# Half of the weight-slice loads of the ternary quantization moved from the SP queue to the ACT queue

## Chip, cores and metric

One Trainium2 chip, 8 cores, one program on all of them. Each core takes half of one of four sequences (2048 tokens and a few at the edges). The metric is the device time in microseconds of the slowest core, as the median over runs.

## The reference

A recurrent attention-like layer and a quantized feed-forward layer, each followed by a layer norm. Cut to what matters here:

```python
# layer 1, x: (4, 4096, 1024)
xp = x @ W_in + b_in
Bx = (xp @ W_B + b_B) @ B_mat            # 16 states
ig, fg = sigmoid(xp @ W_ig + b_ig), sigmoid(xp @ W_fg + b_fg)
h_t = fg_t * h_{t-1} + ig_t * Bx_t       # scan over 4096 tokens
y = tanh(hs @ C_mat + xp @ W_D + b_D) @ W_out + b_out + xp
x = layernorm(x + layernorm(y) * gamma + beta)
# layer 2: w1 (4096, 1024), w2 (1024, 4096)
def weight_quant(w):                     # ternary
    scale = 1.0 / clip(mean(abs(w)), 1e-5)
    return clip(round(w * scale), -1, 1) / scale
def act_quant(x): ...                    # to 8 bits, a scale for each token
h = silu(depthwise_conv(act_quant(x) @ weight_quant(w1).T))
x = layernorm(x + act_quant(h) @ weight_quant(w2).T)
```

The change lies in `weight_quant`: every core computes the mean of |w| of both matrices and then their ternary form.

## The kernel before

The kernel keeps a list of operations in program order (`Prog`). Each operation names its engine and the regions it reads and writes; `finalize_and_emit` works out the semaphore waits and writes one instruction stream for each engine, in program order. A wait stands in the stream of the engine that issues the operation, a DMA's too, so a DMA issued from ACT waits, and makes ACT wait, at its place among ACT's own computations. `load` (L242) issues on the SP queue unless it is told another; `store` (L246) issues on the ACT queue. SP computes nothing.

There are three stages with a barrier between them.

**Stage A** (to about 640 us). First the weights of the gates are folded (to 125 us). Then a loop over 16 *gate slices* of 256 tokens: an SP load of `xgf` (1 MB, two buffers), ACT makes its bf16 part `xgh` (L594), DVE the remainder `xgl` (L598), PE does 24 matmuls into `ps_g`, ACT evicts three gates (L615, L619, L623). At the end of each gate slice, `pump_p1(9)` puts in nine steps of the generator `tern_all`, which quantizes w1 and w2. After the loop come the scan and what the barrier waits for.

`tern_all` has four parts, 98 steps in all:

- `tern_pass1` over w1: 16 items of 128 x 2048 floats (1 MB each) and a step for the mean
- `tern_pass1` over w2: 32 items of 128 x 1024 floats (0.5 MB) and a step for the mean
- `tern_pass2` over w1: 16 items, the same data loaded again, and stored as bf16 (0.5 MB)
- `tern_pass2` over w2: 32 items, stored as bf16 (0.25 MB)

Item i uses load buffer `twf[i % 4]`, and scratch buffers `tu`, `tk16` and `tb` number i % 2. In pass 1 the sum of |w| of an even item is made by ACT (L447, into `tcol0`), that of an odd item by DVE (L452); after each, DVE adds it to a running sum (L460, L464), in order. In pass 2 an even item goes ACT `tu` (L533), DVE `tk16` (L537), ACT `tb` (L540), store from ACT (L247). An odd item goes DVE `tu` (L544), DVE `tk16` (L548), ACT `tb` (L551), store from ACT. The load of item i waits until item i - 4 has read its buffer. Since SP does nothing else, it issues a load as soon as that has happened, up to four items ahead of the computation.

With nine steps to a gate slice, pass 1 runs in gate slices 0 to 5 and pass 2 in gate slices 5 to 10. Slices 11 to 15 have no quantization in them.

**Stage B** (to about 1400 us) is the attention part, **stage C** the feed-forward part, which loads the ternary weights that stage A stored.

Of the kernel before, what the change touches and what calls it, by code (L numbers as in the profile page):

```python
# [184 lines left out]
def build_nc(debug=False):  # L185
# [150 lines left out]
    for fc in range(8):  # L336
# [3 lines left out]
        for j in range(8):  # L340
# [4 lines left out]
             i=ps_pre[:, po:po + 16], fc=fc:  # L345
# [91 lines left out]
    def tern_pass1(src, nrows, width, mean_out, mean_rg, tg,  # L437
                   ps_hbuf, ps_rg, scol):
        stag = f"tcol{scol}"
        slices = tern_slices(nrows, width)  # L440
        for i, (rc, c0, c1) in enumerate(slices):
            wv = c1 - c0
            pr = i % NTB
            twf, tu = twfs[pr], tus[pr]
            load(twf[:, 0:wv], src[rc * 128:(rc + 1) * 128, c0:c1], f"twf{pr}")
            if i % 2 == 0:
                p.op("ACT", lambda twf=twf, tu=tu, e=wv: A.activation(  # L447
                    tu[:, 0:e], twf[:, 0:e], AF.Abs, accum_out=tcol[:, 0:1]),
                     reads=(f"twf{pr}",), writes=(f"tu{pr % 2}", "tcol0"))
                acc, arg = "tcol0", 0  # L450
            else:
                p.op("DVE", lambda twf=twf, e=wv: V.tensor_reduce(  # L452
                    tcol[:, 3:4].rearrange("p (t o) -> p t o", o=1),
                    twf[:, 0:e].rearrange("p (t e) -> p t e", t=1),
                    AX, OP.add, apply_absolute_value=True),
                     reads=(f"twf{pr}",), writes=("tcol3",))
                acc, arg = "tcol3", 3
            ac = 6 + (i % 4)
            if i < 4:
                p.op("DVE", lambda ac=ac, a=arg: V.tensor_copy(  # L460
                    tcol[:, ac:ac + 1], tcol[:, a:a + 1]),
                     reads=(acc,), writes=(f"tcol{ac}",))
            else:
                p.op("DVE", lambda a=arg, ac=ac: V.tensor_add(  # L464
                    tcol[:, ac:ac + 1], tcol[:, ac:ac + 1], tcol[:, a:a + 1]),
                     reads=(acc, f"tcol{ac}"), writes=(f"tcol{ac}",))
            yield
        nun = len(slices)
        p.op("DVE", lambda: V.tensor_add(tcol[:, 6:7], tcol[:, 6:7],
                                         tcol[:, 7:8]),  # L470
             reads=("tcol6", "tcol7"), writes=("tcol6",))
        if nun > 2:
            p.op("DVE", lambda: V.tensor_add(tcol[:, 8:9], tcol[:, 8:9],
                                             tcol[:, 9:10]),
                 reads=("tcol8", "tcol9"), writes=("tcol8",))
            p.op("DVE", lambda: V.tensor_add(tcol[:, 6:7], tcol[:, 6:7],
                                             tcol[:, 8:9]),
                 reads=("tcol6", "tcol8"), writes=("tcol6",))
        p.op("DVE", lambda: V.tensor_scalar(tcol[:, 1:2], tcol[:, 6:7],
                                            1.0 / (nrows * 128 * width), None,  # L480
                                            OP.mult),
             reads=("tcol6",), writes=("tcol1",))
        mm("parsum" + tg, ps_hbuf[0:1, 0:1], s_onesc[:], tcol[:, 1:2],
           reads=("s_onesc", "tcol1"), wr=ps_rg, start=True, stop=True)
        p.op("DVE", lambda: V.tensor_copy(tcol[0:1, 1:2], ps_hbuf[0:1, 0:1]),
             reads=(ps_rg,), writes=("tcol1",))
        mm("parbc" + tg, ps_hbuf[0:128, 0:1], s_ones1[:], tcol[0:1, 1:2],
           reads=("s_ones1", "tcol1"), wr=ps_rg, start=True, stop=True)
        p.op("DVE", lambda: V.tensor_copy(tcol[:, 1:2], ps_hbuf[0:128, 0:1]),
             reads=(ps_rg,), writes=("tcol1",))  # L490
        p.op("DVE", lambda: V.tensor_scalar_max(mean_out[:], tcol[:, 1:2], 1e-5),
             reads=("tcol1",), writes=(mean_rg,))
        p.op("DVE", lambda mo=mean_out, sc=scol: V.reciprocal(
            tcol[:, sc:sc + 1], mo[:]),
             reads=(mean_rg,), writes=(stag,))
        yield

    def tern_pass2(src, dst_hbm, nrows, width, tg, scol):
        stag = f"tcol{scol}"
        slices = tern_slices(nrows, width)  # L500
        for i, (rc, c0, c1) in enumerate(slices):
            wv = c1 - c0
            pr = i % NTB
            twf, tu, tk16, tb = twfs[pr], tus[pr], tk16s[pr], tbs[pr]
            load(twf[:, 0:wv], src[rc * 128:(rc + 1) * 128, c0:c1], f"twf{pr}")
            if SAFE_ROUND:
                p.op("DVE", lambda twf=twf, tu=tu, e=wv: V.tensor_scalar(
                    tu[:, 0:e], twf[:, 0:e], tcol[:, scol:scol + 1], None,
                    OP.mult),
                     reads=(f"twf{pr}", stag), writes=(f"tu{pr % 2}",))  # L510
                p.op("DVE", lambda tu=tu, e=wv: V.tensor_copy(tk[:, 0:e],
                                                              tu[:, 0:e]),
                     reads=(f"tu{pr % 2}",), writes=("tk",))
                p.op("DVE", lambda tu=tu, e=wv: V.tensor_sub(trr[:, 0:e],
                                                             tu[:, 0:e],
                                                             tk[:, 0:e]),
                     reads=(f"tu{pr % 2}", "tk"), writes=("trr",))
                p.op("DVE", lambda e=wv: V.tensor_scalar(tcp[:, 0:e], trr[:, 0:e],
                                                         0.5, None, OP.is_gt),
                     reads=("trr",), writes=("tcp",))  # L520
                p.op("DVE", lambda tu=tu, e=wv: V.scalar_tensor_tensor(
                    tu[:, 0:e], trr[:, 0:e], -0.5, tcp[:, 0:e], OP.is_lt,
                    OP.subtract),
                     reads=("trr", "tcp"), writes=(f"tu{pr % 2}",))
                p.op("DVE", lambda tu=tu, e=wv: V.tensor_sub(tu[:, 0:e],
                                                             tk[:, 0:e],
                                                             tu[:, 0:e]),
                     reads=(f"tu{pr % 2}", "tk"), writes=(f"tu{pr % 2}",))
                p.op("DVE", lambda tu=tu, tb=tb, e=wv: V.tensor_scalar(
                    tb[:, 0:e], tu[:, 0:e], 1.0, -1.0, OP.min, OP.max),  # L530
                     reads=(f"tu{pr % 2}",), writes=(f"tb{pr % 2}",))
            elif i % 2 == 0:
                p.op("ACT", lambda twf=twf, tu=tu, e=wv: A.activation(  # L533
                    tu[:, 0:e], twf[:, 0:e], AF.Identity,
                    scale=tcol[:, scol:scol + 1]),
                     reads=(f"twf{pr}", stag), writes=(f"tu{pr % 2}",))
                p.op("DVE", lambda tu=tu, tk16=tk16, e=wv: V.tensor_scalar(  # L537
                    tk16[:, 0:e], tu[:, 0:e], 1.49, -1.49, OP.min, OP.max),
                     reads=(f"tu{pr % 2}",), writes=(f"tk16{pr % 2}",))
                p.op("ACT", lambda tk16=tk16, tb=tb, e=wv: A.activation(  # L540
                    tb[:, 0:e], tk16[:, 0:e], AF.Copy),
                     reads=(f"tk16{pr % 2}",), writes=(f"tb{pr % 2}",))
            else:
                p.op("DVE", lambda twf=twf, tu=tu, e=wv: V.tensor_scalar(  # L544
                    tu[:, 0:e], twf[:, 0:e], tcol[:, scol:scol + 1], 1.49,
                    OP.mult, OP.min),
                     reads=(f"twf{pr}", stag), writes=(f"tu{pr % 2}",))
                p.op("DVE", lambda tu=tu, tk16=tk16, e=wv: V.tensor_scalar(  # L548
                    tk16[:, 0:e], tu[:, 0:e], -1.49, None, OP.max),
                     reads=(f"tu{pr % 2}",), writes=(f"tk16{pr % 2}",))  # L550
                p.op("ACT", lambda tk16=tk16, tb=tb, e=wv: A.activation(  # L551
                    tb[:, 0:e], tk16[:, 0:e], AF.Copy),
                     reads=(f"tk16{pr % 2}",), writes=(f"tb{pr % 2}",))
            store(dst_hbm[rc * 128:(rc + 1) * 128, c0:c1], tb[:, 0:wv],
                  (f"tb{pr % 2}",), f"q{tg}{rc}_{c0}")
            yield
# [31 lines left out]
    for sl in range(T // GSL):  # L588
        c0 = sl * GSL
# [1027 lines left out]
```

How the kernel before makes its waits and increments, by code:

```python
                def body(handle, eng=eng, idxs=idxs):  # L164
                    for i in idxs:
                        o = ops[i]
                        for sh, val in waits_l[i]:
                            handle.wait_ge(sh, val)
                        instr = o["fn"]() if o["fn"] is not None else handle.nop()
                        if o["sem"] is not None:
                            instr.then_inc(o["sem"][1], 16 if o["dma"] else 1)
                    if eng == "SP":
                        for e2 in ENGINES:
                            if cnt.get(e2, 0):
                                handle.wait_ge(chain[e2], cnt[e2])
                        for j in range(NDMA):
                            if dcnt[j]:
                                handle.wait_ge(dpool[j], dcnt[j])
```

## Time and profile before

| | us |
|---|---|
| median of 2 runs | 2471.48 |
| the two runs | 2469.33, 2473.63 |
| the profiled execution | 2487.02 |
| its slowest core's span (core 7) | 2485.5 |
| shortest span of a core in it (core 2) | 2442.4 |

The profile is of one execution, on its slowest core. Busy over the whole span: PE 55%, DVE 45%, ACT 35%, POOL 5%. These are averages over three stages with different limits; the change touches stage A alone, so the rows that count are those of 125 to 606 us. A row of the stretch view gives each engine's busy time in a stretch with the number of instructions in brackets, the granted TensorE clock as a share of 2.4 GHz, the mean busy share of the 16 DMA engines and what they moved. A row of the time-ordered view gives start, duration, engine (ACTq and SPq are the issue of a DMA from that engine's stream), line, operation, out<-in, and in square brackets how long the engine had been idle and who ended that.

### The profile page before, as it was taken

How to read it: one execution, taken by the hardware profiler on the slowest of the kernel's cores; microseconds unless marked ns; L12 is line 12 of the kernel's file. 1: busy time of each engine (PE TensorE's matmuls, PEld its weight loads, DVE VectorE, ACT ScalarE, POOL GpSimd, SP SyncE). 2: the span in 40 equal slices, each digit the busy share in tenths (PEclk: the TensorE clock that was granted, in tenths of full speed). 3: DMA queues.
4: the chain of work that ended last, by engine and by line, in shares of the span. 5: the costliest groups of instructions: out<-in, count | busy, mean ns of one | idle time of the engine just before them, and what ended most of it. 6: DMA issues, size and time to landing. Idle time of an engine off the chain costs nothing.

```text
span 2485.5 us, 30418 instructions; the slowest of 8 cores (2442.4 to 2485.5 us)
## 1 busy us (share of the span) xinstructions
PE 1368.9 (55%) x9255; PEld 975.5 (39%) x9255; DVE 1117.6 (45%) x2440; ACT 869.4 (35%) x1552; POOL 130.0 (5%) x62
## 2 busy tenths in 40 slices
PE   6711100103009688687887880155758669576565
PEld 6711100103008576575665660133435335343332
DVE  1024323232202433433433434288678686787752
ACT  0023344442111222222222121157447464474551
POOL 0000000000340100101001002000000000000000
PEclk9975555556559898998998995578879767798778
DMA  5376676562350110200100001631010010111010
GB/s 124 103 257 227 223 252 234 172 207 60 102 126 28 48 39 22 60 31 30 52 22 31 30 27 43 195 111 26 18 34 29 24 51 18 35 35 35 26 35 26
DMA packets 132967, 201.71 MB, mean 81 GB/s; under 512 B 46184, under 2 KB 95465, under 8 KB 127624
## 3 DMA queue, kind: packets, MB, share of 16 engines
q1 hardware_dynamic: 114120, 144.92, 20.0%
q10 hardware_dynamic: 18688, 54.85, 6.1%
q8 instruction: 78, 1.28, 0.2%
q14 instruction: 81, 0.66, 0.1%
HBM read 152.52 MB, written 38.03 MB: 77 GB/s over the span
## 4 chain that ended last, share of the span: by engine, by line
PE 38%; DVE 21%; DMA 15%; ACT 12%; issue 7%; POOL 4%; SPq 2%; ACTq 1%; DVEq 1%; POOLq 0%
PE ps_a L261 17%; PE ps_o L261 9%; PE ps_m L261 6%; DVE pmax L1351 5%; PE ps_g L261 3%; DMA xgf<-xg_fm 3%; DMA w1q_hbm<-tb 2%; DMA w2q_hbm<-tb 2%; PE ps_pre L261 2%; ACT sc_a L1102 2%; DVE hbuf L1325 2%; DMA wtr<-W_B_T 2%; POOL xtm L907 2%; DVE xgl L598 1%; DVE sc_a L1120 1%
## 5 line engine op out<-in xcount | busy, mean ns | idle before, releaser
L261 PE MATMUL ps_m<-r1qg,w1q 128*128 128x258 bf16 (+2 forms) x2304 | 314.3, 283 | 101.3 <-DVE hbuf L1325 61.2
L261 PE MATMUL ps_o<-w2q,hq_b 128*128 128x512 bf16 (+1 forms) x1088 | 302.2, 417 | 44.0 <-DVE ps_s L1447 23.8
L261 PEld LDWEIGHTS ps_m<-r1qg,w1q 128*128 128x128 bf16 x2304 | 219.7, 104 | 212.8 <-issue 151.3
L1102 ACT ACTIVATE sc_a<-hbuf,s_convb,s_convw 128x256 f32<-128x256 f32 (+2 forms) x288 | 165.4, 574 | 356.9 <-DVE hbuf L1325 336.5
L261 PE MATMUL ps_a<-pA_h,Win_hi 128*128 128x256 bf16 (+1 forms) x512 | 148.2, 289 | 215.0 <-ACT pA_h L753 140.8
L261 PE MATMUL ps_g<-xgh,WG_hi 128*80 128x256 bf16 x128 | 50.7, 396 | 347.0 <-ACT xgh L594 347.0
L261 PE MATMUL ps_a<-pB_h,WD_hi 128*128 128x256 bf16 (+1 forms) x512 | 150.3, 294 | 57.1 <-ACT pB_h L779 35.7
L261 PEld LDWEIGHTS ps_o<-w2q,hq_b 128*128 128x128 bf16 (+1 forms) x1088 | 109.4, 103 | 155.5 <-issue 86.7
L261 PEld LDWEIGHTS ps_g<-xgh,WG_hi 128*80 128x80 bf16 x128 | 22.4, 175 | 353.1 <-issue 350.8
L1325 DVE SCALAR_TENSOR_TENSOR hbuf<-ps_m,dqs 128x258 f32<-128x258 f32 (+2 forms) x288 | 113.4, 394 | 100.9 <-PE ps_m L261 96.3
L261 PE MATMUL ps_a<-pA_l,Win_hi 128*128 128x256 bf16 (+1 forms) x512 | 147.9, 289 | 7.2 <-DVE pA_l L757 7.2
L261 PE MATMUL ps_a<-pB_l,WD_hi 128*128 128x256 bf16 (+1 forms) x512 | 150.1, 293 | 1.1 <-DVE pB_l L783 1.1
L261 PE MATMUL ps_a<-pB_h,WD_lo 128*128 128x256 bf16 (+1 forms) x512 | 149.7, 292 | 0.0
L261 PE MATMUL ps_a<-pA_h,Win_lo 128*128 128x256 bf16 (+1 forms) x512 | 147.6, 288 | 0.0
L261 PEld LDWEIGHTS ps_a<-pA_h,Win_hi 128*128 128x128 bf16 x512 | 52.6, 103 | 231.2 <-issue 222.1
L261 PE MATMUL ps_a<-pA_h,Wout_hi 128*128 128x256 bf16 (+1 forms) x512 | 139.4, 272 | 2.6 <-DVE zS L843 2.6
L261 PE MATMUL ps_a<-pA_l,Wout_hi 128*128 128x256 bf16 (+1 forms) x512 | 139.4, 272 | 0.0
L261 PE MATMUL ps_a<-pA_h,Wout_lo 128*128 128x256 bf16 (+1 forms) x512 | 139.0, 271 | 0.0
L1120 DVE SCALAR_TENSOR_TENSOR sc_a<-hbuf,s_convw,sc_a 128x256 f32<-128x256 f32 (+2 forms) x288 | 129.1, 448 | 14.3 <-ACT sc_a L1102 13.9
L1108 ACT ACTIVATE sc_d<-hbuf,s_convw 128x256 f32<-128x256 f32 (+2 forms) x288 | 135.1, 469 | 0.0
L1128 DVE TENSOR_TENSOR sc_d<-sc_d,sc_a 128x256 f32<-128x256 f32 (+2 forms) x288 | 114.2, 396 | 31.1 <-DVE sc_a L1120 1.4
L1351 DVE TENSOR_REDUCE pmax<-hbuf 128x256 f32<-128x8192 f32 (+1 forms) x9 | 124.1, 13787 | 0.4 <-ACT hbuf L1132 0.4
(199 smaller groups left out, 2370.6 us busy)
## 6 DMA issues: line engine op xcount, KB each, us to landing
twf<-w1t_f SPq DMA_DIRECT2D x32, 1024.0 KB, 13.5
twf<-w2t_f SPq DMA_DIRECT2D x64, 512.0 KB, 5.9
xgf<-xg_fm SPq DMA_DIRECT2D x16, 1024.0 KB, 10.3
wtr<-W_B_T SPq DMA_DIRECT2D x16, 512.0 KB, 4.4
w1q_hbm<-tb ACTq DMA_DIRECT2D x16, 512.0 KB, 6.6
w2q_hbm<-tb ACTq DMA_DIRECT2D x32, 256.0 KB, 4.9
xtm<-x_tm ACTq DMA_DIRECT2D x16, 512.0 KB, 3.4
r_hbm<-z_tm ACTq DMA_DIRECT2D x16, 512.0 KB, 2.6
```

The lines of the kernel that those rows point to most:

```text
L261: PE.matmul(o, l, r, start=st, stop=sp),
L598: V.tensor_sub(xgl[:], xgf[:], xgh[:]),
L907: p.op("GP", lambda e=uw: GP.tensor_add(xtm[0:e, :], xtm[0:e, :], s_betb[0:e, :]), reads=("xtm", "s_betb"), writes=("xtm",))
L1102: A.activation(sc_as[mm_ % 2][:, 0:e], h[:, c0:c0 + e], AF.Identity, bias=s_convb[:, mm_:mm_ + 1], scale=s_convw[:, 32 + mm_:33 + mm_]),
L1108: A.activation(sc_ds[mm_ % 2][:, 0:e], h[:, c0 + 1:c0 + 1 + e], AF.Identity, scale=s_convw[:, 64 + mm_:65 + mm_]),
L1120: V.scalar_tensor_tensor(sc_as[mm_ % 2][:, 0:e], h[:, c0 - 1:c0 - 1 + e], s_convw[:, mm_:mm_ + 1], sc_as[mm_ % 2][:, 0:e], OP.mult, OP.add),
L1128: V.tensor_add(sc_ds[mm_ % 2][:, 0:e], sc_ds[mm_ % 2][:, 0:e], sc_as[mm_ % 2][:, 0:e]),
L1325: V.scalar_tensor_tensor(o, i, 1.0, d, OP.mult, OP.mult),
L1351: p.op("DVE", lambda e=fw, c0=co: V.tensor_reduce(pmax[:, 0:e].rearrange("p (t o) -> p t o", o=1), hbuf[:, :].rearrange("p (c t) -> p t c" ...
```

## The change

Both `load` calls of the quantization, in pass 1 and in pass 2, get a queue that alternates with the item: even items are loaded from SP as before, odd items from ACT. Which engine computes what, the buffers, the stores and everything else stay.

```diff
@@ tern_pass1
-            load(twf[:, 0:wv], src[rc * 128:(rc + 1) * 128, c0:c1], f"twf{pr}")
+            load(twf[:, 0:wv], src[rc * 128:(rc + 1) * 128, c0:c1], f"twf{pr}",
+                 q=("SP", "ACT")[i % 2])
             if i % 2 == 0:
                 p.op("ACT", lambda twf=twf, tu=tu, e=wv: A.activation(
@@ tern_pass2
-            load(twf[:, 0:wv], src[rc * 128:(rc + 1) * 128, c0:c1], f"twf{pr}")
+            load(twf[:, 0:wv], src[rc * 128:(rc + 1) * 128, c0:c1], f"twf{pr}",
+                 q=("SP", "ACT")[i % 2])
             if SAFE_ROUND:
```

`SAFE_ROUND` is False. 48 of the 96 loads move: 16 of 1 MB (8 in each pass) and 32 of 0.5 MB (16 in each pass).

## Rows read from the trace of the kernel before

**Rows 1.** Stretch view of core 7: from:to, length, PE, PEld, DVE, ACT, POOL, clock, DMA

```profile
100.00:620.00 520.00, 96.25 (x500) 80.32 (x499) 154.65 (x190) 188.03 (x186) 0.00 (x0) 0.60 0.61 198
303.50:414.00 110.50, 10.74 (x48) 8.60 (x48) 33.78 (x26) 53.17 (x32) 0.00 (x0) 0.53 0.73 240
414.00:554.00 140.00, 15.35 (x72) 12.31 (x72) 39.69 (x51) 62.10 (x61) 0.00 (x0) 0.54 0.64 210
730.00:1400.00 670.00, 530.78 (x4319) 422.10 (x4320) 241.60 (x601) 149.89 (x328) 57.82 (x25) 0.90 0.13 37
1400.00:2485.00 1085.00, 669.40 (x4114) 402.47 (x4111) 687.14 (x1589) 513.41 (x1016) 23.22 (x10) 0.78 0.15 45
```

**Rows 2.** Waits in 100 to 620 us: us in total, times, longest

```profile
ACT xgh L594 <- DMA xgf<-xg_fm: 32.5, 6, 14.0
...
SPq L168 <- ACT tu L533: 158.1, 22, 17.7
```

**Rows 3.** View of tile tb: ACT's idle time before it, and times

```profile
  DMA w1q_hbm<-tb: 31.6, 9
  DMA w2q_hbm<-tb: 28.9, 10
```

**Rows 4.** DMA issues with us to landing: 300:414, 414:554, 554:606, then fastest twf

```profile
twf<-w1t_f SPq DMA_DIRECT2D x12, 1024.0 KB, 11.7
...
twf<-w2t_f SPq DMA_DIRECT2D x28, 512.0 KB, 5.6
...
xgf<-xg_fm SPq DMA_DIRECT2D x3, 1024.0 KB, 5.9
...
DMA to landing us min/median/max: 3.8/7.0/18.1
```

**Rows 5.** Time-ordered view, pass 2 over w1: ACT, with one line of DVE

```profile
386.33 2.00 ACT L533 ACTIVATE tu<-twf,tcol 128x2048 f32<-128x2048 f32 x1 [0.51 <-ACT tb L551]
389.76 1.91 ACT L540 ACTIVATE tb<-tk 128x2048 bf16<-128x2048 int16 x1 [1.43 <-DVE tk L537]
391.74 0.33 ACTq L247 DMA_DIRECT2D w1q_hbm<-tb  x1
...
408.95 1.28 DVE L544 TENSOR_SCALAR tu<-twf,tcol 128x2048 f32<-128x2048 f32 x1
...
414.07 1.15 ACT L533 ACTIVATE tu<-twf,tcol 128x1024 f32<-128x1024 f32 x1 [0.51 <-ACT tb L551]
```

**Rows 6.** Time-ordered view, pass 2 over w2: ACT, then DVE

```profile
430.00 1.15 ACT L533 ACTIVATE tu<-twf,tcol 128x1024 f32<-128x1024 f32 x1 [0.50 <-ACT tb L551]
...
433.17 0.33 ACTq L247 DMA_DIRECT2D w2q_hbm<-tb  x1
433.65 1.06 ACT L551 ACTIVATE tb<-tk 128x1024 bf16<-128x1024 int16 x1 [0.56 <-DVE tk L548]
...
435.21 1.91 ACT L594 ACTIVATE xgh<-xgf 128x2048 bf16<-128x2048 f32 x1 [0.50 <-ACT tb L551]
...
445.69 1.15 ACT L533 ACTIVATE tu<-twf,tcol 128x1024 f32<-128x1024 f32 x1
...
431.86 0.75 DVE L544 TENSOR_SCALAR tu<-twf,tcol 128x1024 f32<-128x1024 f32 x1
432.71 0.69 DVE L548 TENSOR_SCALAR tk<-tu 128x1024 int16<-128x1024 f32 x1
```

**Rows 7.** Chain that ended last, pass 1 over w2: start, length, what

```profile
213.87 1.16 ACT tu L447 x2
215.29 1.23 DVE tcol L452
...
231.03 2.30 DVE xgl L598
...
240.13 1.16 ACT tu L447 x2
...
260.20 2.30 DVE xgl L598
```

## The prediction

> **What bounds the kernel now.** I read the stretch view first. From 730 us on PE is busy 531 of 670 us, and then DVE 687 of 1085 [rows 1]; the change has no instruction there. From 100 to 620 us no engine is near full: ACT 188 of 520 us, DVE 155, PE 96, the DMA engines 0.61 of the time [rows 1]. Such a stretch is set by latencies in series. Everything in it passes through ACT in program order: a gate slice, nine quantization items, the next gate slice. So whatever ACT waits for lengthens stage A, and stage B can't begin sooner, because of the barrier. That is how the rest is read: as a sum over ACT's stream.
>
> Then the waits. SP's stream waits 158 us for ACT's `tu` alone [rows 2]: SP stands ready, with free issue time, and is held by buffers. The load queue is not what is scarce. In pass 2 ACT's `tb` waits 31.6 us in the w1 part and 28.9 us in the w2 part for earlier stores to land [rows 3], and over the stage ACT waits 32.5 us for `xgf` [rows 2]. These are all the DMA waits that a better spread of transfers could win back here.
>
> **What the change does to an odd item.** Before, the load of item i went out when item i - 4 was done, three to four items ahead. Now it stands in ACT's stream directly behind ACT's work on item i - 1, so it can't go out earlier than that. There is no cost in the buffer wait, since item i - 4 is long done; the cost is that the lead is gone.
>
> *Pass 2.* ACT's stream for a pair is now: `tu` (even), `tb` (even), store, load (odd), `tb` (odd), store. The last `tb` needs DVE's two operations on the odd item, and these need the load that ACT issued one instruction before. So one whole landing time L is exposed in every pair, with nothing to cover it: DVE has only that item, and behind the waiting `tb` on ACT are its store, the next even item, and the next gate slice with PE behind it.
>
> The pair over w1, from [rows 5]: the even half takes 386.33 to 392.07 (`tu`, DVE, `tb`, and the store's issue, 391.74 + 0.33), 5.7 us. Then the load's issue and L. Then the odd half, from DVE's start at 408.95 to the next `tu` at 414.07, 5.1 us. With 0.2 us for hand-overs that is 11.0 + L. For w2 from [rows 6]: the even half 430.00 to 433.50, 3.5 us; the odd half 0.75 + 0.69 on DVE, 1.06 for `tb`, 0.33 for the store, and five hand-overs of 0.1, 3.3 us; with the hand-over to the load 6.9 + L.
>
> *How long L is.* No load was ever issued so late before, so it is bounded. A load of 0.5 MB landed in 3.8 us at the fastest [rows 4]; the DMA engines moved 240 GB/s at a share of 0.73 and 210 at 0.64 [rows 1], 329 GB/s when busy, so 0.5 MB more is 1.6 us. For w1 (1 MB): 3.8 + 1.6 = 5.4 alone, where a lone `xgf` of the same size took 5.9 [rows 4]. In front of it in ACT's queue is the even item's store, 0.5 MB, 1.6 us, and part of SP's next even load, issued some 4 us before, is still moving, 0.7 us by my choice: L = 7.7. For w2: 3.8, the store of 0.25 MB 0.8, the remainder of SP's load 0.6: L = 5.2. The bounds are the transfer alone (5.4 and 3.8) and the median of before with up to four loads in the queue (11.7, and 5.6 plus the store's 0.8, 6.4) [rows 4]. I stay near the low end, as far fewer loads are in flight.
>
> *The sum for pass 2.* The w1 part now takes 110.5 us with two gate slices in it, the w2 part 140 with three [rows 1]. A gate slice holds ACT from 435.21 to 445.69, 10.5 us [rows 6]; I take 11 for each of the five that fall into pass 2, an estimate from that row, and leave them unchanged. Left are 88.5 us for 8 pairs of w1 (11.1 each) and 107 for 16 of w2 (6.7 each). After: 8 x (11.0 + 7.7) = 150, that is +61; 16 x (6.9 + 5.2) = 194, that is +87. The waits for stores vanish in this, because a store now has the whole exposed landing to land in: their 60 us are inside the numbers before and not counted again.
>
> *Pass 1.* Here ACT isn't blocked by an odd load, as DVE reduces the odd items. But an even item's result slot `tcol0` is free only when DVE has added the item before, and DVE takes that addition in order, behind the odd reduction. So ACT gets one pair ahead at most, and two odd loads are in flight instead of a full four buffers. I followed two gate slices over w2, with 1.16 us for ACT's sum, 1.23 for DVE's [rows 7] and a landing of 5 us, 6 when `xgf` moves too. When the first item after the gates is odd (before: 213.87 to `xgl` at 231.03, 17.2 us [rows 7]): its load goes out at 0 and is reduced by 6.3, the odd loads go out at 0, 1.7, 7.9, 10.0 and 16.6, and the last is reduced at 22.8, where `xgl` can start: +5.7. When it is even (240.13 to 260.20, 20.1 us [rows 7]): odd loads at 1.3, 2.9, 9.1 and 11.1, the last reduced at 18.7, the last even item summed at 18.2, `xgl` at 20.3: nothing lost, since the ninth item no longer waits for an odd load. There are two odd starts over w2 (+11); one slice with 1 MB items and an odd start, where one landing of 7.7 us and the 2 to 3 us of a larger reduction behind it come out at +9; the remaining four items and the mean before pass 2 +4; the even starts 0. Together +24. `xgf` goes out behind fewer loads, but `xgl` and `xgh` wait behind the odd items then, so its earlier landing wins nothing. Bounds: 0, if the shorter `xgf` flights repay the odd starts, and twice as much, 48, if ACT and DVE fall into full alternation.
>
> *The issues.* A DMA issue takes 0.33 us of ACT's stream [rows 5]. In pass 2 the 24 are inside the pair (the hand-overs); in pass 1 the 24 fall into ACT's waiting. After gate slice 10 everything is as before, with the DMA engines only emptier.
>
> **Sum.** 61 + 87 + 24 = +172 us. Against the profiled execution: 2487 + 172 = 2659. The median of the runs shown is 15.5 us below that execution, so 2471.5 + 172 = 2643.
>
> The Trainium skill (DMA: Bandwidth & Descriptors, Rules for kernel authors) says that spreading DMAs over SP, ACT and GpSimd doesn't help bandwidth, since all run on the same 16 DMA engines, and that it only saves the sequencer's issue time. By it the best to be had is SP's issue time, which SP's waits show to be spare; by it alone the time would stay near 2471. The rows of both queues in [rows 1] agree so far: the rate when busy is the same 329 GB/s in both parts of pass 2. The same table's rule, to issue a DMA early and wait for it late, speaks against the change.
>
> **Rivals.**
>
> *Only the issuing queue changes (about 2471, within 2%).* The loads would stay hidden and the DMA engines do the same work. It needs ACT to reach each odd load at least 5 us before DVE needs its data. For it: in pass 1 with an even start that holds. Against it: in pass 2 ACT's next instruction depends on that load. It decides only if pass 2's exposed landing is below (88.5 / 8 - 11.0), 0.1 us, for w1, and below 0 for w2; 3.8 us was the fastest. Chance 0.05.
>
> *Two queues move the data sooner (faster, about 2380).* If transfers from two queues overlap so well that `xgf` no longer queues behind quantization loads and stores no longer behind them either, ACT would win up to 32.5 + 31.6 + 28.9 = 93 us [rows 2, 3]: 2378. For it: the waits are there, and DMA was only 0.6 to 0.7 busy. Against it: each win is smaller than the landing exposed in the same pair. It decides only where L is below the waits per pair, 31.6 / 8 = 4.0 and 28.9 / 16 = 1.8. Chance 0.03.
>
> *Fast landings (slower, but about 2560).* Lone transfers land at the low bounds, 5.4 and 3.8 us, and pass 1 loses nothing: 8 x 16.4 = 131 (+43), 16 x 10.7 = 171 (+64), so +107, 2578; with landings 1 us faster still, 24 less, 2554. For it: the DMA engines have little else to do then. Against it: the store is always just in front. Chance 0.14.
>
> *Slow landings (about 2718).* With 11.7 and 6.4 us: 8 x 22.7 = 182 (+93), 16 x 13.3 = 213 (+106), pass 1 +48: +247. For it: two queues share each DMA engine, and the even load of 1 MB may take half the rate. Chance 0.10, most of it below that value.
>
> **How the numbers follow.** The forecast case, +107 to +247, has 0.68. The median then is 2643; the range is that of the bounds, 2578 to 2718, cut to 2580 to 2710, with about half of the two outer landing cases in it. A change of about 2% (49 us) is what a measurement of this kernel can tell from none. Slower by more has the forecast, the fast and the slow landings, 0.92; within 2% 0.05; faster 0.03.
>
> **What would show it.** In the profile of the changed kernel: `tb` of L551 waits for the landing of `twf`, or for a DVE operation that does, in all 24 pairs; DVE idle before L544 by 5 to 8 us each; the waits for stores before L540 gone; pairs of about 19 and 12 us; gate slices 11 to 15 as long as before; DMA share in pass 2 down by a third or more; stages B and C as long as before, merely later. I would be wrong if ACT issued the odd loads while waiting for something else, if L were under 4 us, or if stage B or C changed length.

## The result

| | before | changed |
|---|---|---|
| median, us | 2474.42 (10 runs) | 2652.71 (11 runs) |
| lowest to highest | 2466.58 to 2527.02 | 2648.25 to 2667.19 |
| slowest core's span in the profiled execution | 2485.5 (core 7) | 2657.3 (core 6) |

The ratio is 1.0728, with a 95% interval of 1.0696 to 1.076: 180 us slower, where +172 us and 2643 were forecast. Here and below, a difference in us is the ratio less 1, times the median of before in the same session (2474.42 here, 2469.12, 2467.43 and 2466.7 in the three sessions of experiments). A few executions fell in a slower state of the chip (2527.02 above is one) and are left out of the ratios, so that of p2_only below rests on two.

### The profile page after: what moved, and what is told of

Its sections match the earlier page's. It is cut to its first block, busy times and chain, and to the rows that moved or that the text cites. A ratio compares the mean times of both kernels' runs of the same rounds, so it can differ in the third digit from the quotient of the medians.

```text
span 2657.3 us, 30308 instructions; the slowest of 8 cores (2635.2 to 2657.3 us)
## 1 busy us (share of the span) xinstructions
PE 1350.7 (51%) x9255; PEld 968.5 (36%) x9255; DVE 1119.4 (42%) x2440; ACT 869.9 (33%) x1552; POOL 130.0 (5%) x62
## 4 chain that ended last, share of the span: by engine, by line
PE 33%; DVE 23%; DMA 17%; ACT 13%; issue 7%; POOL 3%; SPq 2%; ACTq 1%; DVEq 1%; POOLq 0%
PE ps_a L261 16%; PE ps_o L261 7%; DMA twf<-w2t_f 5%; DVE pmax L1353 5%; PE ps_m L261 4%; DMA twf<-w1t_f 3%; PE ps_g L261 3%; ACT sc_a L1104 2%; PE ps_pre L261 2%; DVE hbuf L1327 2%; DVE sc_a L1122 2%; DMA xgf<-xg_fm 1%; DMA wtr<-W_B_T 1%; POOL xtm L909 1%; DVE xgl L600 1%
## 5 line engine op out<-in xcount | busy, mean ns | idle before, releaser
L261 PE MATMUL ps_m<-r1qg,w1q 128*128 128x258 bf16 (+2 forms) x2304 | 300.2, 274 | 111.0 <-DVE hbuf L1327 70.0
L261 PE MATMUL ps_o<-w2q,hq_b 128*128 128x512 bf16 (+1 forms) x1088 | 288.8, 403 | 43.4 <-DVE ps_s L1449 23.3
L261 PEld LDWEIGHTS ps_m<-r1qg,w1q 128*128 128x128 bf16 x2304 | 211.4, 101 | 214.3 <-issue 148.7
```

The costliest lines, as they stand in the source:

```text
L261: PE.matmul(o, l, r, start=st, stop=sp),
```

## The profile after

Line numbers are two or so higher than before: L535 is `tu`, L542 and L553 are `tb` of an even and an odd item, L546 and L550 DVE's two operations on an odd item, L596 `xgh`, L600 `xgl`.

The stretch view of core 6, with the boundaries at the first `xgh`, the first `tu` over w1, the first over w2, the first `xgh` after the quantization, and the end of the gate slices (columns as in [rows 1]):

```profile
133.90:321.70 187.80, 30.45 (x148) 24.80 (x148) 57.89 (x84) 54.22 (x72) 0.00 (x0) 0.58 0.64 211
321.70:495.90 174.20, 10.81 (x52) 8.71 (x52) 36.99 (x36) 53.16 (x32) 0.00 (x0) 0.51 0.46 151
495.90:724.70 228.80, 14.66 (x72) 11.80 (x72) 41.14 (x51) 62.06 (x60) 0.00 (x0) 0.52 0.41 130
724.70:776.80 52.10, 23.38 (x120) 19.17 (x120) 11.46 (x5) 16.52 (x20) 0.00 (x0) 0.66 0.24 66
```

The w1 part of pass 2 went from 110.5 to 174.2 us, the w2 part from 140 to 228.8 [rows 1]. ACT's busy time in them hardly moved (53.17 to 53.16 and 62.10 to 62.06), and the DMA engines, which carry the same bytes, fell from a share of 0.73 to 0.46 and from 0.64 to 0.41. No engine has more to do; there is only more waiting.

ACT in the time-ordered view, one pair over w1 and one over w2, and under them DVE's two operations on an odd item:

```profile
478.12 2.00 ACT L535 ACTIVATE tu<-twf,tcol 128x2048 f32<-128x2048 f32 x1 [0.51 <-ACT tb L553]
481.55 1.91 ACT L542 ACTIVATE tb<-tk 128x2048 bf16<-128x2048 int16 x1 [1.43 <-DVE tk L539]
483.54 0.33 ACTq L247 DMA_DIRECT2D w1q_hbm<-tb  x1
483.89 0.46 ACTq L243 DMA_DIRECT2D twf<-w1t_f  x1
493.49 1.91 ACT L553 ACTIVATE tb<-tk 128x2048 bf16<-128x2048 int16 x1 [10.04 <-DVE tk L550]
...
544.19 1.15 ACT L535 ACTIVATE tu<-twf,tcol 128x1024 f32<-128x1024 f32 x1
546.23 1.06 ACT L542 ACTIVATE tb<-tk 128x1024 bf16<-128x1024 int16 x1 [0.89 <-DVE tk L539]
547.36 0.33 ACTq L247 DMA_DIRECT2D w2q_hbm<-tb  x1
547.72 0.46 ACTq L243 DMA_DIRECT2D twf<-w2t_f  x1
554.28 1.06 ACT L553 ACTIVATE tb<-tk 128x1024 bf16<-128x1024 int16 x1 [6.99 <-DVE tk L550]
...
490.78 1.29 DVE L546 TENSOR_SCALAR tu<-twf,tcol 128x2048 f32<-128x2048 f32 x1 [9.32 <-DMA twf<-w1t_f]
492.17 1.23 DVE L550 TENSOR_SCALAR tk<-tu 128x2048 int16<-128x2048 f32 x1
```

The load goes out at 483.89, the line after the store. DVE, idle for 9.32 us, starts when it has landed, and ACT's next computation starts 10.04 us after its last one ended. Compare [rows 5], where the odd item's data lay ready. How much of this there is, by the view of waits in 320 to 725 us (two lines) and by the view of the tile `tb` (its last line here):

```profile
DVE tu L546 <- DMA twf<-w2t_f: 118.8, 16, 10.7
DVE tu L546 <- DMA twf<-w1t_f: 85.5, 8, 14.5
...
  DVE tk L550: 209.3, 24
```

All 24 odd items wait, and ACT with them, 209.3 us. No wait for a store is left among ACT's waits before `tb`; before, it was 60 us [rows 3].

The chain that ended last shows the landings (start, length, what), four of those over w2 and the two first over w1:

```profile
330.58 6.09 DMA twf<-w1t_f
...
347.68 7.51 DMA twf<-w1t_f
...
547.72 4.82 DMA twf<-w2t_f
...
559.37 4.71 DMA twf<-w2t_f
...
571.27 8.63 DMA twf<-w2t_f
...
586.73 5.00 DMA twf<-w2t_f
```

The eight of w1 take 5.3 to 11.9 us, 7.9 in the mean; the sixteen of w2 3.7 to 9.0, 5.6 in the mean.

In pass 1 the view of waits gives what ACT waited for, before (first three lines, core 7, 130 to 310 us) and after (core 6, 134 to 322 us):

```profile
ACT tu L447 <- DMA twf<-w2t_f: 23.7, 8, 4.1
ACT tu L447 <- DMA twf<-w1t_f: 18.0, 4, 5.2
ACT tu L447 <- DVE tcol L464: 1.6, 4, 0.4
...
ACT tu L448 <- DVE tcol L465: 38.8, 11, 5.4
ACT xgh L596 <- DMA xgf<-xg_fm: 35.0, 6, 12.3
ACT tu L448 <- DMA twf<-w2t_f: 6.0, 4, 2.9
ACT tu L448 <- DMA twf<-w1t_f: 5.7, 1, 5.7
```

The wait for the slot `tcol0`, which DVE frees only behind its odd reduction, grew from 1.6 to 38.8 us, and part of the waits for ACT's own loads, which were there before, went.

## The experiments

The theory: a load costs what of its landing is exposed, and moving it into ACT's stream made the odd loads late (*lateness*). The rival: a load costs because it is issued from ACT and shares the DMA engines with SP's, wherever it stands (*queue*). Each kernel was timed against the one before in three rounds. The stage times below are from ACT's time-ordered view, as in the last section, each the median of the eight cores of one profiled execution.

| kernel | ratio, 95% interval | us | pass 1 | pass 2, w1 | pass 2, w2 |
|---|---|---|---|---|---|
| before | | | 161.0 | 106.3 | 140.2 |
| changed | 1.0728 (1.0696 to 1.076) | +180 | 189.1 | 174.3 | 228.2 |
| p1_only | 1.0084 (1.0059 to 1.0108) | +21 | 185.8 | 110.8 | 139.4 |
| p2_only | 1.06 (1.0546 to 1.0655) | +148 | 158.6 | 169.7 | 224.2 |
| p2_quarter | 1.0321 (1.0298 to 1.0344) | +79 | 162.8 | 142.0 | 182.9 |
| p2_sp_late | 1.0439 (1.0405 to 1.0474) | +108 | 164.8 | 150.7 | 203.3 |
| act_lead1 | 1.0159 (1.014 to 1.0178) | +39 | 177.1 | 118.3 | 160.8 |
| act_lead3 | 1.0078 (1.0048 to 1.0108) | +19 | 173.3 | 108.4 | 139.7 |
| load_then_store | 1.0574 (1.051 to 1.0637) | +142 | 187.6 | 148.2 | 205.5 |
| xgf_early_after | 1.0682 (1.0642 to 1.0723) | +168 | 182.9 | 172.3 | 223.7 |
| xgf_early | 0.9938 (0.992 to 0.9957) | -15 | 146.4 | 105.0 | 138.7 |
| xgf_early_lead3 | 0.9976 (0.9956 to 0.9996) | -6 | 158.4 | 107.6 | 139.0 |
| tb4 | 0.9811 (0.9771 to 0.9851) | -47 | 159.3 | 89.4 | 116.5 |
| xgf_early_tb4 | 0.9759 (0.9715 to 0.9802) | -59 | 147.7 | 88.7 | 116.2 |

### One pass alone

`p1_only` has the first of the change's two edits, `p2_only` the second.

> Only the odd loads of pass 1 are issued from ACT; pass 2 is as before. Theory (lateness: a load costs what of its landing stands exposed behind ACT's work): +24 us, about 2498, range 2485 to 2515, with the first gate slices after an odd start longer and the even starts unchanged. Rival (queue: a load costs because it is issued from ACT and shares the DMA engines with SP's, wherever it stands): 24 of the 48 moved loads and half of the bytes, so half of the loss of 178 us, +89, about 2563.

> Only the odd loads of pass 2 are issued from ACT; pass 1 is as before. Theory (lateness): 64 us for w1 and 89 for w2, +153, about 2627, range 2610 to 2645, DVE's L544 waiting for the landing in all 24 pairs. Rival (queue): half of the loss, +89, about 2563.

They cost 21 and 148 us, in sum 169 of the 180, and each leaves the other pass's stages nearly as they were. The loads of the same 24 odd items were moved in each, with the same bytes. So it is not the moved load that costs but where its consumer stands: in pass 1 ACT mostly goes on, in pass 2 it waits. The rival's +89 for each lies outside both intervals.

### Half of the late loads

```diff
 # pass 2 only
-            load(..., f"twf{pr}")
+            load(..., f"twf{pr}", q=("SP", "SP", "SP", "ACT")[i % 4])
```

> Pass 2 only, and only items 3, 7, 11 and so on are loaded from ACT: 12 late loads, 4 over w1 and 8 over w2. Theory (lateness): cost by exposed landings, 12 of 24, half of the 153 us of pass 2: +77, about 2551; a little more if SP's remaining loads make landings longer. If instead a store wait that the late load had swallowed stays in the other pairs, nothing changes in that sum, since it is in the time of before too. Rival (queue): a quarter of the moved loads, +45, about 2519.

+79. Over w1 four late loads cost 142.0 - 106.3 = 36 us, 8.9 each; the eight of the changed kernel 68, 8.5 each. Over w2 it is 43 for eight, 5.3 each, against 88 for sixteen, 5.5 each. The cost goes with the count of exposed landings.

### The same place without ACT's queue

```diff
 # pass 2 only
-            load(..., f"twf{pr}")
+            load(..., f"twf{pr}", q="SP", reads=(("tb0",) if i % 2 else ()))
```

> No load is issued from ACT. In pass 2 the load of an odd item stays on SP but also waits until ACT has made the bf16 tile of the item before it, the place at which ACT would issue it. Theory (lateness): the same landing is exposed, less the 24 issues of 0.4 us in ACT's stream: +130 to +155, about 2615. Rival (queue, or ACT's issue time): nothing is issued from ACT, so the time of before, 2474, within 15 us.

With no load on ACT, pass 2 is slow all the same: +108 us. That is what the rival can't have. But it is less than I expected. The time-ordered view of ACT, core 3, shows where the load stood (SP issued it at 354.09, beside the store):

```profile
348.68 2.00 ACT L534 ACTIVATE tu<-twf,tcol 128x2048 f32<-128x2048 f32 x1
352.11 1.91 ACT L541 ACTIVATE tb<-tk 128x2048 bf16<-128x2048 int16 x1 [1.43 <-DVE tk L538]
354.09 0.36 ACTq L247 DMA_DIRECT2D w1q_hbm<-tb  x1
363.37 1.91 ACT L552 ACTIVATE tb<-tk 128x2048 bf16<-128x2048 int16 x1 [9.35 <-DVE tk L549]
...
365.78 2.00 ACT L534 ACTIVATE tu<-twf,tcol 128x2048 f32<-128x2048 f32 x1 [0.51 <-ACT tb L552]
```

The pair takes 17.1 us. The load had no store ahead of it in its own queue and no issue in ACT's stream, and SP's next even load went out behind it instead of ahead. Whether the place behind the store made the difference is asked next.

### Load ahead of the store, both on ACT

```diff
 # pass 2, even item i; the odd item's own load is left out
                  reads=(f"tk16{pr % 2}",), writes=(f"tb{pr % 2}",))
+            if i % 2 == 0:
+                tern_load(src, slices, i + 1, "ACT")
             store(dst_hbm[...], tb[:, 0:wv], ...)
```

`tern_load` is the load of item j, as a function.

> The changed kernel with one swap in pass 2: ACT issues the load of the odd item just ahead of the store of the even item, instead of just behind it. Theory (a store ahead of the load in the queue is part of the exposed landing, 1.6 us over w1 and 0.8 over w2, and the store's issue of 0.4 us too): 8 x 2.0 + 16 x 1.2 = 35 us less than the changed kernel, about 2615, range 2605 to 2630. This would also explain why the late load on SP cost only 108 us. Rival (the late load on SP was cheaper because it was on SP): no change by the swap, 2650.

+142, 38 us less than the changed kernel, though the interval of this ratio alone is 16 us wide to each side. So the place behind the store cost something. Its stages over w1 and w2 (148.2, 205.5) come out like those with the late load on SP (150.7, 203.3). Over w1 the swap won 26 / 8 = 3.3 us a pair, more than the 2.0 expected. ACT's view, core 6, shows what I had missed:

```profile
382.15 1.91 ACT L549 ACTIVATE tb<-tk 128x2048 bf16<-128x2048 int16 x1 [1.43 <-DVE tk L546]
382.17 0.34 ACTq L243 DMA_DIRECT2D twf<-w1t_f  x1
384.14 0.33 ACTq L247 DMA_DIRECT2D w1q_hbm<-tb  x1
392.44 1.91 ACT L560 ACTIVATE tb<-tk 128x2048 bf16<-128x2048 int16 x1 [8.38 <-DVE tk L557]
```

The load is issued at 382.17, 0.02 us after `tb` began and while it computes for 1.91 us. ACT's stream issues a DMA beside a running computation; what held the load back in the changed kernel was the store ahead of it, which waits for `tb` to end.

The two kernels reach like stages by different ways, as the landings in the chain show (the late load on SP, core 3, then this kernel, core 6):

```profile
354.09 6.47 DMA twf<-w1t_f
...
382.17 7.47 DMA twf<-w1t_f
```

Over all cores, in the pairs with no gate slice inside (those that all these kernels have in common), the median landing is 8.4 us over w1 and 5.1 over w2 in the changed kernel, 7.6 and 5.2 in p2_only, whose pass 2 is the same, 7.9 and 5.8 here, and 6.6 and 4.5 with the late load on SP. So the swap did not shorten the landing by the 1.6 and 0.8 us that the expectation gave to the store ahead in the queue; it won because the load goes out 2.3 us earlier over w1 and 1.5 over w2. The late load on SP goes out only 0.4 us earlier, but lands sooner. Whether that is SP's queue, the store in the other queue, or the even load that no longer stands ahead, no run separates.

### One and three items of lead

```diff
 # act_lead1: at the start of an even item, in both passes; none at the odd item
+            if i % 2 == 0:
+                tern_load(src, slices, i, "SP")
+                tern_load(src, slices, i + 1, "ACT")
 # act_lead3: item 1 at the start of the pass, then at the end of an even item
+            if i % 2 == 0:
+                tern_load(src, slices, i + 3, "ACT")
```

> Both passes: the odd load is issued from ACT ahead of the even item's work instead of behind it, so with one item of lead. Theory (lateness): each pair of pass 2 gets the even half as cover, 5.7 us of a landing of 8 over w1 and 3.5 of 5.5 over w2: 8 x 5.7 + 16 x 3.5 = 102 us less than the changed kernel, and up to 15 more from pass 1: about 2545, range 2530 to 2560. Rival (queue): about 2653.

> Both passes: the odd loads are issued from ACT at the same places of its stream as in the changed kernel, but each is the load of the odd item after next (three items ahead) instead of the next one. Same queue, same number of issues, same bytes. Theory (lateness): two items of cover are 17 us in w1 and 10 in w2, more than a landing of 8 and 5.5, so nearly the whole loss goes: 2474 to 2500, the upper end from 24 issues of 0.4 us in ACT's stream in pass 2 and some in pass 1. Rival (queue): nothing gets better, about 2653.

These keep the queue, the bytes and the number of issues, and change the lead. With three items of lead the 180 us are down to 19, and pass 2 is as fast as before (108.4 and 139.7, against 106.3 and 140.2). With one item it is +39, which is 141 us less than the changed kernel, where I had expected 102 to 117. A pair over w1 gained (174.3 - 118.3) / 8 = 7.0 us, not 5.7, a pair over w2 4.2, not 3.5. ACT-issued w1 loads landed in 7.0 us in the median, against 8.0 in the changed kernel, which accounts for 1 of the 1.3; two of the 24 loads had a gate slice for cover too. The rest, and all of the 0.7 over w2, I haven't split further.

Most of what act_lead3 keeps is in pass 1, 173.3 against 161.0. There its trace shows longer waits: in the mean of the eight cores ACT waits 25.9 us for `xgf` after the first slice (17.7 before) and 38.1 for its own loads (30.3 before). The issues take 8.5 us of ACT's stream in all. I can't say whether the issues or the lead of three where SP had four is behind it; no run separates them.

### The gate input, earlier

```diff
 # at slice sl, ahead of pump_p1(9); the load at the head of the slice stays for sl = 0
+        if sl + 1 < T // GSL:
+            load_fm(xgfs[1 - pr], GSL, xg_fm[:, c0 + GSL:c0 + 2 * GSL], f"xgf{1 - pr}")
```

> The kernel before with one edit: the load of the gate input for the next slice is put ahead of the nine quantization items in program order, so it stands in SP's queue in front of their loads. All loads on SP. Theory: ACT's waits for xgf (32.5 us of the kernel before, 6 times) go, less what the quantization loads then land later: 2445 to 2460. Rival (the stretch is bound by the DMA engines): no change, 2474.

> The early load of the gate input together with odd loads on ACT three items ahead. If a second queue has any use, it is here, since SP's order no longer holds the gate input back. Theory (lateness): near the run with the early gate input alone, within 20 us, 2445 to 2475. Rival (two queues move data sooner): below it by 20 us or more.

> The changed kernel with the load of the gate input put ahead of the nine quantization items in program order. Theory (in the changed kernel the one w2 landing in four that takes 8 to 9 us instead of 4 to 5 shares the DMA engines with the 1 MB gate input; early, the gate input competes with the first odd load of the group instead): the long landings move but stay, and pass 1 loses its waits for the gate input: 2630 to 2655. Rival (the gate input was only a victim of the queue): the long landings vanish too, 3 us each in some 8 places, 2615.

On the kernel before it gains 15 us, all in pass 1 (161.0 to 146.4). Joined with the ACT loads three items ahead it gains 6: the second queue brought nothing, and cost in pass 1 again what it cost alone. On the changed kernel the difference is 12 (180 less 168, from two sessions), which is not clear of noise: the intervals of the two ratios overlap. Its question was about the long landings: of the sixteen over w2 in the changed kernel four take 8.2 to 9.0 us, the other twelve 4.5 in the mean. SP's stream issued `xgf` at 497.50, 568.97, 627.96 and 689.20, and the long ones are the loads issued next, 1.9 to 2.3 us later. One of them in the view of issues, 571.3 to 579.9 us of the changed kernel (the mean rate, and the shares of the SP queue, q1, and the ACT queue, q10):

```profile
DMA packets 1457, 2.30 MB, mean 267 GB/s; under 512 B 64, under 2 KB 1088, under 8 KB 1457
...
q1 hardware_dynamic: 1169, 1.51, 60.8%
q10 hardware_dynamic: 288, 0.79, 22.8%
```

2.3 MB moved while the load of 0.5 MB landed; 1.51 of it was SP's. With the gate input a slice earlier in SP's order the long landings were still there, at the same place of each group, since SP stands ready to issue it at that same moment, one slice earlier: 9.46, 9.41 and 9.80 us at 565, 625 and 686 us. I had expected them to move to the first odd load, which they didn't; that they stay, as a share of the DMA engines taken by 1 MB more, held.

### Four store buffers

```diff
-        _tb = tuple(SB(f"tb{i}", [128, TW], BF16, stack=tstack) for i in range(2))
-        tbs = (_tb[0], _tb[1], _tb[0], _tb[1])
+        tbs = tuple(SB(f"tb{i}", [128, TW], BF16, stack=tstack) for i in range(NTB))
 # and the regions f"tb{pr % 2}" become f"tb{pr}"
```

> The kernel before with four tb buffers instead of two, so that ACT need not wait for the store two items back. Theory (pass 2 of the kernel before is latency in ACT's stream): the 60 us of waits for stores shrink to what the DMA engines still ask for: w1 moves 25 MB in 110 us where 329 GB/s would need 82, w2 29 MB in 140 where the compute pair of 5.2 us and three gate slices need 115: 35 us less at most, 2435 to 2455. Rival (the stores were late because the DMA engines were full): the same waits come back as waits for loads, 2467.

> Both edits to the kernel before: the early gate input and four tb buffers, all loads on SP. Theory: the early input wins in pass 1 and the buffers in pass 2, so they add up: 15 + 12 to 35 us, 2420 to 2445, the fastest of all. Rival (both use up the same idle time of the DMA engines): no better than the better one alone.

If pass 2 was latency in ACT's stream, the wait that the stores make in the kernel before must be worth its length. It was, and more than I expected: -47 us. The expectation's own bounds (28 us over w1, 25 over w2) add up to 53, and its 35 was too timid. (Its 82 us for w1 doesn't follow from its 25 MB, which at 329 GB/s need 76; [rows 1] give 240 GB/s in 110.5 us, 26.5 MB, so 81. The part took 89.4.) The w1 part now moves data nearly all the time, the w2 part takes 116.5 us, where the compute pairs and gate slices alone need 115. The stretch view of core 7:

```profile
303.50:392.00 88.50, 10.64 (x48) 8.53 (x48) 33.31 (x27) 51.26 (x32) 0.00 (x0) 0.54 0.90 301
392.00:509.00 117.00, 16.12 (x73) 12.77 (x73) 39.48 (x52) 62.83 (x60) 0.00 (x0) 0.54 0.71 244
```

The DMA share over w1 is 0.90, with SP as the only queue for loads, where the change had brought it to 0.46. With the early gate input it is -59 us (2407.68 against 2466.7, ratio 0.9759), the fastest kernel here and below the 2420 to 2445 expected, by the same timid bound; the two gains add up, 13 in pass 1 and 42 in pass 2 by the table.

A second queue of another engine, GpSimd's, was not tried, nor were ACT's loads with a lead joined with the four store buffers.

## Why the prediction was right

**The place.** Stages B and C were to keep their length: from 638.89 us to the end before, from 808.38 in the changed kernel, 1846.6 and 1848.9 us. Gate slices 11 to 15 take 52.0 and 52.1 us. All of the loss lies in the quantization.

**Pass 2 over w1.** Forecast 8 x (11.0 + 7.7) and +61; measured +63.7 in the two profiled cores (174.2 against 110.5), +68 by the medians over cores. The pair at 371.54 to 391.13 us is 19.6 long, with a landing of 8.6: 11.0 + L. The mean landing was 7.9. The 7.7 was right as a sum, but its parts aren't shown: it gave 1.6 us to the store in front, and with the store behind (load_then_store) the landing stayed at about 8. That the parts came out at the right sum is in part luck.

**Pass 2 over w2.** Forecast 16 x (6.9 + 5.2) and +87; measured +89. The pair at 544.19 to 555.84 is 11.65, with 4.8 of landing: 6.8 + L. L was 5.6 in the mean. My remainder of 0.6 us for SP's traffic was right for none of them: twelve took 4.5 us, less than I gave, and four 8.7, because of the gate input, which I had left out of this term. Three landed in less than the 4 us that were named as a sign of being wrong (3.7 to 3.9); the mean didn't.

**DVE's idle time.** 5 to 8 us were forecast before each L544. It was 10.7 over w1 and 7.4 over w2 in the mean (85.5 / 8 and 118.8 / 16), since DVE is idle from its last operation on the even item, and so through `tb` and the store's issue as well as L.

**Pass 1.** Forecast +24; measured +21.6 in the two profiled cores, +28 by the medians, +21 for the pass alone. Slice by slice, from one `xgl` to the next in the chain of the changed kernel:

```profile
135.95 2.30 DVE xgl L600
...
177.09 2.30 DVE xgl L600
...
213.63 2.30 DVE xgl L600
...
243.62 2.30 DVE xgl L600
...
273.21 2.30 DVE xgl L600
...
303.52 2.30 DVE xgl L600
```

The steps are 41.1, 36.5, 30.0, 29.6 and 30.3 us. Before they were 39.5, 26.9, 25.4, 29.2 and 26.0 (two of the `xgl` are in [rows 7]), so the differences are +1.6, +9.6, +4.6, +0.4 and +4.3, where 0, +9, +5.7, 0 and +5.7 were worked out: the odd starts pay, the even ones don't. The tail before pass 2 gave +0.8 instead of +4.

The mechanism, ACT held by `tcol0`, is in the trace, but the sum left terms out. The mean over the eight cores of ACT's wait for that slot rose by 25 us (10.4 to 35.7), its wait for `xgf` after the first slice by 8 (17.7 to 25.5), where nothing was forecast, and that for its own loads fell by 13 (30.3 to 17.3). "These are all the DMA waits" was wrong: on core 7 ACT's `tu` waited 41.7 us for loads in pass 1, and no rival counted them. That +24 came so near owes something to terms that cancel.

**Where a step was loose.** It said that the load "can't go out earlier" than ACT's work on the item before. load_then_store shows that ACT issues a DMA beside running work; what it can't pass is a wait ahead of it in the stream. In pass 2 that is the store's wait, so the sum stood; in a kernel without a store there, the rule as I put it would have been 1.9 us too dear for each pair over w1. And the rows of [rows 1] don't tell the two queues apart, as the prediction has it; they give both together.

**The rivals.** *Only the queue changes* and *two queues move the data sooner* both needed hidden landings. act_lead3 hides them, and then the first of the two is nearly what happens: within 2%, +19 us. Even there nothing was gained: with the landings hidden, the w1 stage on two queues took 108.4 us and on one 106.3. The Trainium skill says this of bandwidth (DMA: Bandwidth & Descriptors, Rules for kernel authors: spreading DMAs over issuing engines doesn't help); these runs agree, and add that the issuing engine's place in the program is what one pays with. The *fast* and *slow landings* were bounds of L, and the measured 7.9 and 5.6 lie inside both.

## What to carry to other kernels

A DMA belongs in the stream of an engine that has nothing to wait for. Put into the stream of a computing engine, a load starts only when that engine's waits ahead of it are over; if the engine's next instruction needs it, its whole landing is paid at every turn (8 x 7.9 + 16 x 5.6 us here), so such a load is written some items ahead (three did here, one still cost 39 us), and ahead of the store that waits, not behind it. When a stage is a sum of latencies, look at which waits recur in the busiest stream: two more store buffers were worth 47 us, a second queue, tried with two store buffers only, nothing.

## What the runs showed of the hardware

- ACT issued a load 0.02 us after it had begun a computation of 1.91 us (load_then_store, 382.15 and 382.17): the issue doesn't wait for the running instruction, only for the semaphores ahead in the stream.
- A load's issue from ACT mostly takes 0.33 to 0.46 us, but 97 of the 384 in the changed kernel, over all cores, took more than 0.6, and one 2.77 (at 396.90, core 6). The first here is a usual one; the second follows SP's issue of `xgf` at 568.97 (changed kernel, ACT's view). The cause is not shown; it can't be the gate input alone, as no `xgf` was issued between 323.78 and 413.00, where the one of 2.77 lies:

```profile
559.37 0.46 ACTq L243 DMA_DIRECT2D twf<-w2t_f  x1
...
571.27 1.66 ACTq L243 DMA_DIRECT2D twf<-w2t_f  x1
```

- One queue was enough for 301 GB/s at a DMA share of 0.90 with 8 KB rows of loads and a second queue of stores (tb4), and a load of 0.5 MB took 4.5 us with no gate input beside it and 8.7 with 1 MB issued about 2 us before on the other queue (changed kernel, means of twelve and of four).
